# Sort's main loop: the code one-hots are split between two engines, and the low carry joins the prefix sums

## The reference, cut to what matters

```
x = layernorm(x + L0(x, edge_index, ...))     # softmax and segment_sum over dst
x = layernorm(x + L1(x, edge_index_t, ...))   # segment_sum over src
x = layernorm(x + L2(x, edge_index, ...))     # softmax and segment_sum over src
x = layernorm(x + L3(x, ...))                 # two rounds of segment_sum over dst
```

## Time and profile before

| | |
|---|---|
| median of three runs | 9235.28 us |
| lowest, highest | 9209.74, 9261.55 us |
| profiled execution, its own time | 9263.73 us |
| its span | 9261.9 us |
| TensorE, weight loads | busy 4890.4, 3981.1 us |
| VectorE, ScalarE, GpSimd | busy 4455.1, 2080.0, 5467.3 us |

### The profile page before, as it was taken

One profiled execution on the slowest core, in us unless ns is written; L12 is line 12 of the kernel. 1 busy time (PEld: TensorE's weight loads), 2 busy tenths in 40 slices (PEclk: granted clock), 3 DMA queues, 4 the chain that ended last, 5 costly groups with the idle time before them and its releaser, 6 DMA issues. The chain is left out here.

```text
span 9261.9 us, 112670 instructions
## 1 busy us (share of the span) xinstructions
PE 4890.4 (53%) x33002; PEld 3981.1 (43%) x33002; DVE 4455.1 (48%) x14979; ACT 2080.0 (22%) x4783; POOL 5467.3 (59%) x5311
## 2 busy tenths in 40 slices
PE   4567767775666663666664555544433334433232
PEld 2344444445556552656662444443233333322222
DVE  8656666645666675223332566555444443211113
ACT  8223333322222223111111111111222222211010
POOL 0345555536676764666663667765466665566665
PEclk9778888877888885555556767766666667655555
DMA  0011111115555552555553667664344443233332
GB/s 18 19 31 35 35 34 35 35 50 138 144 148 146 149 138 55 118 119 117 119 117 101 194 194 206 193 183 123 88 140 137 138 140 114 74 93 94 90 95 79
DMA packets 1304018, 990.43 MB, mean 107 GB/s; under 512 B 287713, under 2 KB 1192995, under 8 KB 1303411
## 3 DMA queue, kind: packets, MB, share of 16 engines
q0 software_dynamic: 183088, 352.33, 14.9%
q1 hardware_dynamic: 700995, 378.63, 14.6%
q10 hardware_dynamic: 419328, 252.26, 10.1%
HBM read 613.75 MB, written 368.79 MB: 106 GB/s over the span
## 5 line engine op out<-in xcount | busy, mean ns | idle before, releaser
L975 POOL DMA_INDIRECT l_rows<-tab,by_src x1664 | 1745.9, 1049 | 908.6 <-issue 488.0
L707 POOL DMA_INDIRECT sorted_dst<-pay,place_i x783 | 830.0, 1060 | 841.9 <-DVE place_i L655 623.3
L975 POOL DMA_INDIRECT l_rows<-tab,by_dst x832 | 948.1, 1140 | 482.5 <-issue 233.5
L975 POOL DMA_INDIRECT l3a_rows<-tab,by_dst x832 | 803.0, 965 | 440.7 <-issue 225.2
L975 POOL DMA_INDIRECT l3b_rows<-tab,by_dst x832 | 797.1, 958 | 421.4 <-issue 238.9
L1422 PE MATMUL l3b_ps_o<-l3b_rows,l3b_sel 128*128 128x128 f32 x1664 | 355.5, 391 | 834.9 <-issue 478.3
L1121 PE MATMUL l_ps_z<-l_win,l_sel_t 128*128 128x128 f32 x3328 | 752.0, 352 | 51.9 <-DMA l_win<-win 16.9
L1422 PEld LDWEIGHTS l3b_ps_o<-l3b_rows,l3b_sel 128*128 128x128 f32 x1664 | 318.3, 290 | 872.4 <-issue 535.6
L1449 DVE TENSOR_SCALAR l3b_sel<-iota,by_dst 128x128 f32<-128x128 f16 x832 | 184.4, 298 | 1002.6 <-DMA lo_rows<-low_rows 861.0
L1121 PEld LDWEIGHTS l_ps_z<-l_win,l_sel_t 128*128 128x128 f32 x3328 | 604.0, 248 | 72.7 <-issue 37.2
L1130 PE MATMUL l_ps_o<-l_val,l_sel 128*128 128x132 f32 (+1 forms) x3328 | 599.5, 339 | 0.0
(11 more groups left out here) (422 smaller groups left out, 12711.4 us busy)
## 6 DMA issues: line engine op xcount, KB each, us to landing
parts<-l_sums ACTq DMA_DIRECT2D x416, 264.0 KB
l_win<-win SPq DMA_DIRECT2D x1664, 64.0 KB
parts<-l3a_sums SPq DMA_DIRECT2D x208, 512.0 KB
l_row<-slot_rows ACTq DMA_DIRECT2D x624, 128.0 KB
parts<-l_sums ACTq DMA_DIRECT2D x208, 272.0 KB
parts<-l3b_sums SPq DMA_DIRECT2D x208, 256.0 KB
low_bc<-lo_rows SPq DMA_DIRECT2D x194, 256.0 KB
l_rows<-tab,by_src POOLq DMA_INDIRECT x1664
```

The source lines that it names most:

```text
L707: pool.indirect_dma_start(sorted_dst, bass.IndirectOffsetOnAxis(ap=place_i[:, 4 * DST + s % 4, g:g + 1], axis=0), pay[:, col(s, g), :], No ...
L975: pool.indirect_dma_start(rows[:, q, g, :], None, table, bass.IndirectOffsetOnAxis(ap=index[:, k * G + g:k * G + g + 1], axis=0))\
```

## The change

- `histogram`: the last product is followed by one more, the identity times `carry_lo` repeated for the eight blocks, added into the same bank. So `prefix` holds the running histograms with the low carry in them. The histogram now waits for `carry_done` of its key.
- `lookup`: the product with `carry_lo` (L373) goes for blocks 1 to 7, since their prefix has it; block 0 keeps it. The wait for `carry_done` goes.
- The carry: the next carry is `carry_hi` (f16) plus the last prefix, which has the low part.
- `carry_hi` is cast by ScalarE after the second half of `same`, and not by VectorE.
- `permuted`: one tensor_tensor compare makes the slot one-hots of the part's four blocks (`slot_at`, 512 elements), then four compares make `tile_at`. The multiplication by `code` is done by ScalarE (`codes`, four activations of 128 columns with a pointer scale, after `carry_hi` and before `lo` of the next unit).
- `permute` waits for ScalarE's `coded` too.

```diff
             def histogram(k, s):
...
-                    mm = pe.matmul(ps_pre[k][:, g:UG], lo[:, b, g], replicate(hi[:, b, g], 1, UG - g),
-                                   start=g == 0, stop=True, skip_group_check=True)
-                mm.then_inc(hist_done[k], 1)
+                    pe.matmul(ps_pre[k][:, g:UG], lo[:, b, g], replicate(hi[:, b, g], 1, UG - g),
+                              start=g == 0, stop=False, skip_group_check=True)
+                pe.wait_ge(carry_done[k], s + 1)
+                pe.matmul(ps_pre[k], ident16[:], replicate(carry_lo[:, b], 1, UG), start=False, stop=True,
+                          skip_group_check=True).then_inc(hist_done[k], 1)
             def lookup(k, s, u):
...
-                pe.wait_ge(carry_done[k], s + 1)
...
                     pe.matmul(out, lo_t[:, b, g], carry_hi[:, b], start=True, stop=False)
-                    pe.matmul(out, lo_t[:, b, g], carry_lo[:, b], start=False, stop=False)
-                    if g:
-                        pe.matmul(out, lo_t[:, b, g], prefix[:, b, g - 1], start=False, stop=False)
+                    pe.matmul(out, lo_t[:, b, g], prefix[:, b, g - 1] if g else carry_lo[:, b], start=False, stop=False)
...
             permute:
+                    pe.wait_ge(coded, n + 1)
...
+            def codes(s, part):
+
+                mine = [g for g in blocks(s) if g // 4 == part]
+                act.wait_ge(slot_oh, s * UG + mine[-1] + 1)
+                for g in mine:
+                    at, n = col(s, g), s * UG + g
+                    act.activation(code_at[:, n % 16], slot_at[:, n % 16], ACT.Copy, scale=code[:, at:at + 1])\
+                       .then_inc(coded, 1)
...
             ScalarE's loop over the units, after the second half of same:
+                act.wait_ge(sum_done[k], s + 1)
+                wait_count(act, base_done[k], s)
+                act.activation(carry_hi[:, 2 * k + 1 - s % 2], carry[:, k, 1 - s % 2], ACT.Copy)\
+                   .then_inc(carry_hi_done[k], 1)
+                if u >= 5:
+                    codes((u - 5) // 2, (u - 1) % 2)
...
             permuted:
-                    dve.tensor_single_scalar(tile_at[:, n % 16], wide[:], split[:, s % 2, 0, g:g + 1], ALU.is_equal)
-                    at = col(s, g)
-                    dve.tensor_scalar(code_at[:, n % 16], wide[:, 0:P], split[:, s % 2, 1, g:g + 1],
-                                      code[:, at:at + 1], ALU.is_equal, ALU.mult).then_inc(perm_oh, 1)
+                wait_count(dve, perm_mm, n1 - 16)
...
+                dve.tensor_tensor(slot_at[:, n0 % 16:n0 % 16 + len(mine)],
+                                  replicate(split[:, s % 2, 1, mine[0]:mine[-1] + 1], 2, P),
+                                  replicate(wide[:, 0:P], 1, len(mine)), ALU.is_equal).then_inc(slot_oh, len(mine))
+                for g in mine:
+                    dve.tensor_single_scalar(tile_at[:, (s * UG + g) % 16], wide[:], split[:, s % 2, 0, g:g + 1],
+                                             ALU.is_equal).then_inc(perm_oh, 1)
...
             tick:
-                    dve.tensor_tensor(carry[:, k, o], carry[:, k, b], prefix[:, 2 * k + b, UG - 1], ALU.add)\
+                    dve.tensor_tensor(carry[:, k, o], carry_hi[:, 2 * k + b], prefix[:, 2 * k + b, UG - 1], ALU.add)\
...
-                if now:
-                    dve.wait_ge(sum_done[k], s + 1)
-                    wait_count(dve, base_done[k], s)
-                    dve.tensor_copy(carry_hi[:, 2 * k + o], carry[:, k, o]).then_inc(carry_hi_done[k], 1)
```

More of the change, by code:

```diff
@@ L204, in sort_edges @@
         zeroed = kit.sem("sort_zeroed")
+        slot_oh, coded = kit.sem("sort_slot_oh"), kit.sem("sort_coded")
         stepped, steps_in, steps_out, rises_done, above_done = (
@@ L382, in permute @@
                 for g in mine:
-                    n = perm0 + s * UG + g
-                    pe.wait_ge(perm_oh, s * UG + g + 1)
+                    n = s * UG + g
+                    pe.wait_ge(perm_oh, n + 1)
+                    pe.wait_ge(coded, n + 1)
                     for h in range(2):
@@ L450, in _ @@
                         act.activation(prefix[:, b], ps_pre[k], ACT.Copy).then_inc(prefix_done[k], 1)
+                act.wait_ge(sum_done[k], s + 1)
[4 more added lines that the diff above has]
+                    codes((u - 5) // 2, (u - 1) % 2)
                 if u + 1 < len(units):
                     lane_hots(*units[u + 1])
+            for u in range(len(units), len(units) + 5):
+                codes((u - 5) // 2, (u - 1) % 2)
             act.wait_ge(perm_mm, UT)
@@ L604, in permuted @@
             def permuted(s, part):
[L606 to L614, removed]
-                    dve.tensor_single_scalar(tile_at[:, n % 16], wide[:], split[:, s % 2, 0, g:g + 1], ALU.is_equal)
-                    at = col(s, g)
-                    dve.tensor_scalar(code_at[:, n % 16], wide[:, 0:P], split[:, s % 2, 1, g:g + 1],
-                                      code[:, at:at + 1], ALU.is_equal, ALU.mult).then_inc(perm_oh, 1)
+                mine = [g for g in blocks(s) if g // 4 == part]
+                n0, n1 = s * UG + mine[0], s * UG + mine[-1] + 1
+                if n0 < 16:
+                    dve.wait_ge(self_mm, perm0)
+                wait_count(dve, perm_mm, n1 - 16)
+                if part == 0:
+                    dve.wait_ge(split_done, 3 * s + 3)
+                dve.tensor_tensor(slot_at[:, n0 % 16:n0 % 16 + len(mine)],
[4 more added lines that the diff above has]
+                                             ALU.is_equal).then_inc(perm_oh, 1)
             def tick(u):
@@ L645, in tick @@
                     dve.wait_ge(carry_hi_done[k], s + 2)
+                    wait_count(dve, base_done[k], s)
                     dve.tensor_tensor(carry_lo[:, 2 * k + o], carry[:, k, o], carry_hi[:, 2 * k + o], ALU.subtract)\
```

## The result

| | before | after |
|---|---|---|
| median, runs | 9222.51 us, 4 | 9449.76 us, 4 |
| lowest, highest | 9192.33, 9261.55 us | 9403.74, 9453.77 us |
| span of the profiled execution | 9261.9 us | 9449.3 us |

The changed kernel takes 1.0223 times as long, 95% interval 1.0191 to 1.0254. Forecast were 9325 us; slower was right, and the size is nearest that of the rival "stuck" (9400). The medians lie 227 us apart, the two profiled spans 187.4: the profiled execution of the kernel before took 9263.73 us, more than any of its four runs. The rows account for the 187.4.

What follows compares the result with a forecast made beforehand. Bound: a chain of waits with late TensorE semaphores around GpSimd's stores. Direct terms -0.29 + 0.3 a round cancel; more long rounds add 0.93 us over 97 rounds, +90: 9235 to 9325 us, range 9165 to 9480.

Steps and rivals of the forecast that it cites:

- rival "stuck": Main loop: no normal round returns, 16.3 and 19.6 us rounds alternate, mean 18.0, +165 us, 9400 us; chance 0.12.
- the bound: Main loop: no engine full, a chain of waits; TensorE's semaphores arrive late, many about 1.2 us after GpSimd's burst of stores.
- R: Start of VectorE's `picked` product in the DST unit; forecast near 3.6 us before the next burst, 3.9 before the change.
- S: Start of GpSimd's burst of eight indirect stores; 15.8 us from one to the next in the normal round read.
- normal rounds: Loop rounds with `prefix` standing before S, about 15.8 us; long ones, `prefix` after S, take 19.7.
- the compares: VectorE's DST tick: slot compare 0.68 us, tick 1.99 against 2.28; gain 0.29 us a round, 28 over 97.
- ScalarE's durations: ScalarE's new work: first multiply 0.4 us, bounds 0.27 to 0.40 each; `carry_hi` 0.2; 1.4 us more per unit.
- the permutation's start behind `prefix`: TensorE's queue: permutation waits for ScalarE's first multiply, starting 1.5 to 1.6 us after `prefix` starts, against 1.1 before.
- the 0.3 us a round of the sum: GpSimd's burst: the slot compare lengthens the second store in the SRC tick; +0.3 us a round, bounds 0 and 0.58.
- no loss from TensorE's part and `carry_hi`: Lookup -0.28 us, new histogram matmul +0.25, net nothing, though `prefix` moves 0.25 later; `carry_hi` off VectorE gives 0.
- the share of long-form equivalents: Main loop: rounds counted as long rise from 13 to 35 in 100; with longer long rounds, +0.93 us a round, +90 us.
- the 0.9 of the forecast: TensorE's transposes come 0.6 us later after R and S 0.3 earlier, so they move 0.9 us against S.

Runs made afterwards that it cites:

- the four edits on the first chip: Changed kernel with permutation one unit later, without multiplies, or with multiplies earlier; kernel before with multiplies and slot compare alone: 0.9927, 0.9953, 0.9959, 1.0162 of the kernel before.
- the lag of six: Changed kernel with TensorE's permutation six units behind instead of five, so it never waits for ScalarE's multiplies: 9364.61 us, 0.9927 of the kernel before.

## Why the prediction was wrong in size

**Right: the bound, with one reservation.** From R to S it is 3.62 us (1213.34 to 1216.96) where 3.6 was forecast, and the loss is in the waits for `place_i` alone. But R does not follow the burst's last store by 1.2 us in either form that is left, as it did in the normal rounds of before: it follows by 1.8 to 2.0 us in the rounds of 16, and by a median of 5.4 in the long ones (5.4 in those of before too). The semaphore that comes about 1 us after the burst is now that of `prefix` or of `lo`, and work stands between it and R.

**Right: the compares.** 683 ns for the slot compare (0.68 taken), 1.99 us from its start to `place_i` (1168.49 to 1170.48) against the 2.28 of the earlier trace rows. The 0.29 us are gained, in each round.

**Right: ScalarE's durations.** 396 ns a multiply (0.40), four in 1.27 us; `carry_hi` 247 ns, 0.05 more than taken. Its line's slope said 0.2; 49 elements have more of a fixed part than the slope shows.

**Right: the permutation's start behind `prefix`.** It starts 1.54 us after `prefix` (1163.94 to 1165.48), 1.5 to 1.6 forecast, 1.1 before.

**Too large, and put on the wrong instruction: GpSimd.** Over all 783 stores the mean is 820.02/783 = 1.047 us, against 829.98/783 = 1.060 before: the 0.3 us a round of the sum were not there. Nor is it the slot compare that holds a store. The 35 stores with 0.2 us or more of it beside them, and neither a `tile_at` nor a `hi` compare, all took 0.97 us. The 59 with 1 us or more of `tile_at` compares beside them, and nothing of the other two, took a median of 1.10 (1205.17, 1.11 us, under 1204.67, 1.46 us). The prediction had read `tile_at` as harmless, from rows in which `code_at` stood between.

**Right: no loss from TensorE's part and `carry_hi`.** With these alone, 0.9953. (The lookup loses seven matmuls, not eight, 24 for 31, since block 0 keeps its `carry_lo`: 0.035 us less than the 0.28 priced.)

**Wrong: "the share of long-form equivalents goes from 13 to 35 in 100".** By the same measure it went to (18.31 - 15.8)/3.9 = 64 in 100, by count to 66 of 97 rounds. The term was +0.93 us a round and measured 2.0. Three things are in it.

The delay itself was taken too small for the place that decides. I had moved the transposes by 0.9 us against S. Behind long rounds `prefix` moved from S + 0.44 to S + 1.87, by 1.43. Of it 0.76 is the permutation's start against R (-0.21 to 0.55; 0.6 forecast), 0.29 the earlier S, 0.17 the way from `lo` to the next `prefix` (2.11 us before, 2.28 after), on which the new histogram matmul stands a second time; I left that out. The rest, about 0.2, is that the permutation ran longer (median 1.97 us before, 2.18 after).

That permutation's length was no term of the forecast, and the clock sets it: 1.57 us at 1.00, 2.71 at 0.57. With it at the higher clock `prefix` stood at S + 1.26, with it at the lower at a median of S + 2.09. So behind a long round the clock decides between a round of 16 us and another long one.

And I treated the delay as a push that tips over some rounds, and chose a share between what was and what could be. But a round's form follows from where `prefix` stands at S, and that from the round before. The delay was larger than what lay between S + 0.44 and the edge at about S + 1.4, so no long round of after, past the first ten, leads back to a normal one, and each of the 27 rounds of 16 us is followed by a long one, since the next `lo` starts after the next S (1217.47 against 1216.96). The numbers for that were in the trace of before: S + 0.44, the 0.9 of the forecast and its 0.25 for the new matmul once more give S + 1.6, past the edge. The rival "stuck", mean round 18.0, was the outcome, at 12 in 100.

With the stores last the change costs 2.16 us a round too. That this is so near to the 2.0 with them is not shown to be of one cause: there the bound goes from VectorE's work to the ring, here the loss goes through the forms of a round.

**Open.** Why TensorE's semaphores come late beside a burst of indirect stores in the first comparison and on the first and third chip, and not on the second, is not told by any view; nor is it shown that the chip itself is what differs. The transposes ahead of the permutation, with the lag of five, met no late semaphores, so the one edit that would test the order of these two alone is missing: that the delay acts through the transposes' place is read from the rounds, while that it comes from the permutation's wait is shown by the four edits on the first chip. Whether the lag of six would also end the 2.16 us with the stores last wasn't tried.

## What to carry to other kernels

When work moves to an idle engine, price the place where it is put in that engine's queue, and the first instruction elsewhere that waits for it: the same four multiplies cost 2% behind the prefix copy, and nothing ahead of it or used one unit later (where semaphores come late; where they do not, the change was only run with the transposes first, and cost 0.45%). Where a loop has more than one form of a round, don't move their share by feel: carry the new delays from one round into the next, at either clock, and see which form it settles in. And try a kernel on more than one chip before a wait is taken for a property of the machine.

## What the runs showed of the hardware

- While GpSimd issues its eight indirect stores, semaphores raised by TensorE can reach other engines late: "remote" idle of 7.53 us before a `lo` whose transposes were long done, ended 0.78 us after the last store. With the stores behind the loop no such wait is left, and the rounds of the changed kernel on the same chip fall from 18.49 to 11.7 us. The Trainium skill (Perfetto Trace Analysis, Tensor Engine Instruction (MATMUL, LD_WEIGHTS)) says that a matmul's end in the trace is estimated, and that its semaphore follows only when PSUM has acknowledged the writes and the update has spread, both outside the window shown. The trace agrees in that no view shows what lies in the 7.53 us. That they lie in this gap, and not elsewhere, is not shown.
- It differs from chip to chip, or with what else differed between those runs: on one of them the kernel before takes 7998.15 us, and with its transposes first GpSimd waits for a place at only three of 783 stores; on the others the kernel before takes 9222.51 to 9415.74.
- Of VectorE's compares some lengthen the indirect store beside them and some do not. `hi` (tensor with tensor, 0.56 us): the store took 1.43 us instead of 0.97 (1162.06). The slot compare (tensor with tensor, 0.68 us): 0.97 in all of 35. `tile_at`, four in a row: a median of 1.10 in 59 (at most 1.20); in the kernel before, where each stands between two `code_at`, a median of 0.97 in 121 (at most 1.05). What makes the difference was not separated.
- With the stores behind the loop TensorE was granted the clock 1.00 throughout (420 to 1300 us), with them in it 0.83 over the loop of both kernels of the first comparison.
